# A Mamba block with projections in split precision: two of the next unit's four x tiles are made in a unit's first part, and the last lowering of g moves into the next unit

## The reference

```python
proj = jnp.einsum('bsd,ed->bse', x, in_proj_w)      # gate 8192 | x 8192, B 1024, C 1024 | dt 128
hBC  = silu(causal_conv(proj_hBC, conv_w, taps=4) + conv_b)
L    = exp(segsum(dt * A))                          # per head, within a chunk
Y_diag = einsum('bzlhn,bzshn,bhzls,bzshp->bzlhp', C, B, L, x * dt)
Y_off  = einsum('bzlhn,bzhpn,bhzl->bzlhp', C, prev_states, exp(A_cum))
y = Y_diag + Y_off + x * D
g = y * silu(gate)
g = g * rsqrt(mean(g * g over a group's 1024 channels) + eps) * norm_w
out = einsum('bsi,oi->bso', g, out_proj_w)
```

## Time and profile before

| what | value |
|---|---|
| median of 3 runs | 1887.01 us |
| profiled execution | 1886.13 us, span 1884.3 us |
| granted TensorE clock, mean | 0.982 |
| PE busy | 1778.5 us, 94% |
| VectorE busy | 1293.8 us, 69% |
| ScalarE busy | 1061.2 us, 56% |
| GpSimd busy | 935.5 us, 50% |
| DMA | 114.14 MB, 61 GB/s |

### The profile page before, as it was taken

The page is one execution under the profiler, slowest core; times in us unless marked ns, Lnnn a source line. Parts: engine busy times, 40 slices in busy tenths (PEclk is TensorE's granted clock), DMA queues, the critical chain, the costliest instruction groups (busy, mean ns, idle before and its releaser), DMA issues.

```text
span 1884.3 us, 31309 instructions
## 1 busy us (share of the span) xinstructions
PE 1778.5 (94%) x9752; PEld 1375.2 (73%) x9752; DVE 1293.8 (69%) x2091; ACT 1061.2 (56%) x1936; POOL 935.5 (50%) x717
## 2 busy tenths in 40 slices
PE   7989999999999999999999999999999999999976
PEld 6867778777777777777777777777777777777755
DVE  4756667666666677766676667666677666766688
ACT  5546555656546566555546565465665555565632
POOL 1325464555445565354645554454654545455563
PEclk9799999999999999999999999999999999999988
DMA  4412121111202121022211212121211212112121
GB/s 175 156 41 71 55 65 49 40 62 53 71 28 71 49 67 50 26 71 59 67 45 44 62 48 71 31 68 49 68 50 31 66 60 65 43 47 62 34 95 56
DMA packets 77162, 114.14 MB, mean 61 GB/s; under 512 B 21441, under 2 KB 28097, under 8 KB 76097
## 3 DMA queue, kind: packets, MB, share of 16 engines
q1 hardware_dynamic: 59424, 80.07, 14.4%
q10 hardware_dynamic: 17568, 31.99, 5.2%
HBM read 88.94 MB, written 23.07 MB: 59 GB/s over the span
## 4 chain that ended last, share of the span: by engine, by line
issue 46%; POOL 34%; PE 9%; DVE 5%; ACT 3%; SPq 1%; DMA 1%; POOLq 1%; ACTq 0%; DVEq 0%
POOL yt L1509 9%; POOL ssq L1504 6%; POOL wg_lo L1440 4%; POOL wo_lo L1440 4%; POOL prev L1490 3%; POOL yt L1512 3%; POOL wx_lo L1440 3%; PE bank L454 2%; PE bank L456 2%; PE bank L455 2%; PE bank L591 1%; PE bank L654 1%; ACT lm L999 0%; DMA acc<-x_dram 0%; DVE bn L1095 0%
## 5 line engine op out<-in xcount | busy, mean ns | idle before, releaser
L1509 POOL TENSOR_TENSOR yt<-yt,ea 128x384 f32<-128x384 f32 (+1 forms) x128 | 189.3, 1479 | 392.4 <-DVE ea L1356 392.4
L1145 DVE SCALAR_TENSOR_TENSOR xc<-bank,bpar,xc 128x511 f32<-128x511 f32 (+2 forms) x384 | 285.7, 744 | 52.7 <-ACT xc L854 48.2
L1326 DVE TENSOR_TENSOR lm<-lm,cbm 128x512 f32<-128x512 f32 x256 | 186.4, 769 | 158.4 <-ACT lm L1002 158.4
L454 PE MATMUL bank<-h_hi,wg_hi 128*128 128x512 f32 x640 | 264.7, 414 | 27.8 <-ACT gate L958 17.6
L456 PE MATMUL bank<-h_hi,wg_lo 128*128 128x512 f32 x640 | 252.5, 395 | 0.0
L455 PE MATMUL bank<-h_lo,wg_hi 128*128 128x512 f32 x640 | 251.9, 394 | 0.0
L454 PE MATMUL bank<-wo_hi,g_hi 128*128 128x512 f32 x496 | 207.7, 419 | 7.2 <-POOL wo_lo L1440 7.2
L1490 POOL TENSOR_TENSOR prev<-prev,dec 128x512 f32<-128x512 f32 x96 | 101.8, 1061 | 221.7 <-DVE prev L1275 130.7
L454 PE MATMUL bank<-h_hi,wx_hi 128*128 128x512 f32 x512 | 210.7, 411 | 0.0
L456 PE MATMUL bank<-h_hi,wx_lo 128*128 128x512 f32 x512 | 201.0, 393 | 0.0
L455 PE MATMUL bank<-h_lo,wx_hi 128*128 128x512 f32 x512 | 200.6, 392 | 0.0
(11 more groups left out here) (180 smaller groups left out, 3836.7 us busy)
## 6 DMA issues: line engine op xcount, KB each, us to landing
raw_w<-w_in_dram SPq DMA_DIRECT2D x145, 256.0 KB, 2.7
raw_w<-w_out_dram SPq DMA_DIRECT2D x64, 256.0 KB, 2.6
part_d<-part ACTq DMA_DIRECT2D x64, 256.0 KB, 2.2
part<-part_d ACTq DMA_DIRECT2D x58, 256.0 KB, 2.7
rt<-rows_d SPq DMA_DIRECT2D x256, 8.0 KB
acc<-x_dram SPq DMA_DIRECT2D x8, 256.0 KB, 6.8
acc<-w_mod_dram SPq DMA_DIRECT2D x2, 1024.0 KB, 6.1
lh<-neg_d SPq DMA_DIRECT2D x128, 8.0 KB
```

The lines of the kernel that those rows point to most:

```text
L454: nc.tensor.matmul(out_ap, whi(k), hhi(k), start=(k == 0), stop=False)
L1145: stt(dst[:, at], ps[:, 0:HALF - 3 + k], w(k), dst[:, at], ALU.mult, ALU.add)\
L1326: tt(lm[:, h % 4, :], lm[:, h % 4, :], cbm[:, toks(hf)], ALU.mult).then_inc(v_m, 1)
L1509: tt(yt[:, j % 2, cols], yt[:, j % 2, cols], ea[:, j % 2, cols], ALU.add).then_inc(p_t3, 1)
```

## The change

The x tiles are projected in the order 2, 3, 0, 1. Tiles 2 and 3 of the next unit are projected, tapped, convolved and put through Silu in the first part of a unit. For this `xc` has six slots instead of four (tiles 2 and 3 alternate), and `prev` four instead of five. Only two x tiles (for c = 3: the four B/C half tiles and two x tiles) stay in the second part. For c > 0, `transposes(0)` comes ahead of gate tile 1. `lower_g` of the last pair is done by VectorE after the second scaling of x in the next unit. The fills' order and their places in the first part change too. The core of the diff, with the parts for the prologue, the indices and the last unit left out:

```diff
-        xc = sb("xc", [128, NCT, HALF])
+        xc = sb("xc", [128, NCT + 2, HALF])
-        prev = sb("prev", [128, NZ + 1, BLOCK])
+        prev = sb("prev", [128, NZ, BLOCK])
...
+        X_ORDER = (2, 3, 0, 1)
+        def x_fill(c, j):
+            return 4 + nth(j) if c == 1 else (16, 17, 20, 21)[nth(j)]
...
         def by_step(todo):
             if len(todo) == 6:
-                return [todo[0:1], todo[1:3], todo[3:4], todo[4:6]]
-            return [todo[z:z + 1] for z in range(4)]
+                return [todo[0:2], todo[2:3], todo[3:5], todo[5:6]]
+            return [todo[0:2], todo[2:3], todo[3:4], []]
...
             if c == 3:
-                return [[("bc", 0), ("bc", 1)], [("bc", 2), ("bc", 3), ("x", 0)], [("x", 1), ("x", 2)], [("x", 3)]]
-            return [[("x", j)] for j in range(NCT)]
+                return [[("bc", 0), ("bc", 1)], [("bc", 2), ("bc", 3)], [("x", 0)], [("x", 1)]]
+            return [[], [("x", 0)], [("x", 1)], []]
...
 TensorE, gate_proj
-                if z == 2:
-                    te.wait_ge(a_gate, 4 * u + (2 if c == 0 else 1))
-                else:
-                    te.wait_ge(v_conv, 4 * u + (2, 3, 0, 4)[z])
+                if z == 0 and c == 0:
+                    te.wait_ge(v_bcconv, 4 * (g + 1))
+                    te.wait_ge(v_conv, 4 * u + 2)
+                elif z == 0:
+                    te.wait_ge(a_ea, 4 * (u - 1) + 1)
+                elif z == 1:
+                    te.wait_ge(v_conv, 4 * u + (3 if c == 0 else 4))
+                elif z == 2 and c == 0:
+                    te.wait_ge(v_conv, 4 * u + 4)
+                elif z == 2:
+                    te.wait_ge(a_gate, 4 * u + 1)
...
+                else:
+                    te.wait_ge(v_conv, 4 * (u + 1) + 1)
...
 TensorE, the unit (before: gates 1 and 2, then per z transposes, out_proj, states, gate 3 at z = 2)
+                def next_work(j):
+                    if c == 3:
+                        if j < 2:
+                            next_bc(2 * j)
+                            next_bc(2 * j + 1)
+                        else:
+                            next_x(j - 2)
+                    elif j < 2:
+                        next_x(j)
+                    elif j == 2:
+                        gate_proj(g, c + 1, 0)
...
                 if c == 0:
                     gate_proj(g, c, 0)
+                    gate_proj(g, c, 1)
                     group_bc()
+                    transposes(0)
+                    transposes(1)
+                else:
+                    transposes(0)
+                    gate_proj(g, c, 1)
+                    transposes(1)
                 gate_proj(g, c, 2)
+                previous(0)
+                states(0)
+                transposes(2)
+                next_x(2)
+                previous(1)
+                states(1)
+                transposes(3)
+                next_x(3)
+                gate_proj(g, c, 3)
+                previous(2)
+                states(2)
+                exp_a(0)
+                diff(0)
+                diff(1)
+                previous(3)
...
 ScalarE, the unit's first part (new order)
+                for f in todo[0]:
+                    unit_fill(f, g)
+                if c == 0:
+                    silu_gate(u, c, 0)
+                silu_gate(u, c, 1)
+                for f in todo[1]:
+                    unit_fill(f, g)
+                silu_gate(u, c, 2)
+                for f in todo[2]:
+                    unit_fill(f, g)
+                if more:
+                    next_tap(("x", 2))
+                part_step(0)
+                if more:
+                    silu_x(u + 1, hv, 2)
+                part_step(1)
+                if more:
+                    next_tap(("x", 3))
+                silu_gate(u, c, 3)
+                if more:
+                    silu_x(u + 1, hv, 3)
...
 ScalarE, second part, behind split_g(j - 1), the taps and the fill of j
+                    if more and c < 3:
                         if j == 2:
+                            silu_x(u + 1, hv, 0)
+                        if j == 3:
+                            silu_x(u + 1, hv, 1)
+                            silu_gate(u + 1, c + 1, 0)
...
 VectorE, the unit's first part (new order)
+                scale_x(0)
+                scale_x(1)
+                if not first:
+                    lower_g(u - 1, (c - 1) % UPG, NCT - 1)
+                    group_sums(u, g1, b1, h1)
+                new_state(0)
+                scale_x(2)
+                previous(0)
+                next_conv(("x", 2))
+                previous(1)
+                new_state(1)
+                scale_x(3)
+                next_conv(("x", 3))
+                previous(2)
+                new_state(2)
```

More of the change, by code:

```diff
@@ L269, in ffn_bank @@
             return (6, 7, 4, 5)[t % 4]
[L271 to L275, removed]
         block = ctx.enter_context(nc.Block())
@@ L609, in exp_a @@
                 def exp_a(j):
-                    if j == 0:
+                    if j == 0 and end:
                         te.wait_ge(a_gate, 4 * u + 3)
+                    elif j == 0:
+                        te.wait_ge(v_conv, 4 * (u + 1) + 2)
                     elif j == 1:
@@ L653, in transposes, with previous @@
                     for j in range(NCT):
-                        lst = nc.tensor.transpose(bank[2 + z % 2][:, j * 128:(j + 1) * 128], xc[:, j, chunk(z)],
+                        lst = nc.tensor.transpose(bank[2 + z % 2][:, j * 128:(j + 1) * 128], xc[:, xslot(hf, j), chunk(z)],
                                                   ident[:, :])
                     lst.then_inc(t_xt, 1)
+                def previous(z):
+                    if first or (end and z > 0):
+                        return
+                    if z == 0 and hf == 1:
+                        te.wait_ge(p_w, filled(g, 3 if c == 1 else 15))
+                    out_proj(u - 1, z)
+                    if z == 0:
+                        if c == 0:
+                            te.wait_ge(v_bl, 2 * g + 1)
+                        if c in (0, 3):
+                            sum_squares(g - 1 if c == 0 else g, 1 if c == 0 else 0)
@@ L1019, in split_g @@
                     act(g_parts(not more)[0][:, j, :], yt[:, j % 2, :], ACT.Copy, scale=par(c // 2, j, NORM)).then_inc(a_hi, 1)
-                    if j == NCT - 1 and not (last and c == 3):
-                        silu_x(u + 1, 3)
                     if c < 2 and j == 0:
@@ L1068, in unit @@
                 split_g(NCT - 1)
+                if more and c == 3:
+                    silu_x(u + 1, hv, 1)
             def group(g, last, first):
@@ L1308, in unit, with previous @@
-                    if end and z == 3:
-                        ve.wait_ge(a_bcsilu, 2 * GROUPS)
-                        for v in range(2):
-                            for k in range(NK):
-                                i = 16 + v * NK + k
-                                ts((ga_row, gb_row)[v][:, k * 128:(k + 1) * 128], ident[:, :], small[:, i:i + 1], None,
-                                   ALU.mult).then_inc(v_diag, 1)
-                items, n = proj_items(c, last), 0
+                def previous(z):
+                    if not first and not (end and z > 0):
+                        accumulate(u, g1, b1, h1, z)
@@ L1318, in unit, with next_conv, lower_g @@
+                items = proj_items(c, last)
                 nv, hv = (nb, 1) if hf == 0 else (nb + 1, 0)
                 pv = (c // 2) if hf == 0 else (c // 2 + 1) % 2
+                def next_conv(item):
+                    if not end:
+                        conv(item, item_bank(c, item), nv, hv, g + 1, pv)
+                def lower_g(v, cv, j):
+                    ve.wait_ge(a_hi, 4 * v + j + 1)
+                    ghi, glo = g_parts(end and cv == c)
+                    if j == 0 and not (end and cv == c):
+                        ge(ve, t_out, 4 * v)
+                    stt(glo[:, j, :], yt[:, j % 2, :], par(cv // 2, j, NORM), ghi[:, j, :].bitcast(F),
+                        ALU.mult, ALU.subtract).then_inc(v_lo, 1)
@@ L1321, in mix @@
+                if end:
+                    ve.wait_ge(a_bcsilu, 2 * GROUPS)
+                    for v in range(2):
+                        for k in range(NK):
+                            i = 16 + v * NK + k
+                            ts((ga_row, gb_row)[v][:, k * 128:(k + 1) * 128], ident[:, :], small[:, i:i + 1], None,
+                               ALU.mult).then_inc(v_diag, 1)
                 def mix(h):
```

255 lines of the change are left out of this document (110 added, 145 removed).

## The result

The changed kernel takes 2096.86 us (median of 4 runs, 2092.37 to 2099.92) against 1885.87 us (4 runs, 1883.68 to 1892.02) of the kernel before on the same chip: 1.111 times as long, 95% interval [1.108, 1.113]. The forecast was 2053 us, the range 1950 to 2105.

The account below looks back on a forecast made before the run. The prediction took TensorE, busy 94% of the span, as the bound, with at most 7.6 us per group to win. It summed 1886 + 132 (waits) + 35 (clock) = 2053 us, range 1950 to 2105.

Parts of the forecast that it names:

- The waits: New TensorE waits at yo, yd, transposes, group_bc and gate 3: 25.5 us per middle group together.
- behind group_bc and ahead of out_proj: In c = 0, 1.0 us of wait for mask products and 1.0 us for the last lowering of g.
- the saved changes of kind: On TensorE, a projection behind another saves 0.1 us; four saved per group, 0.4 us.
- the largest term: For c > 0, transposes wait 4.0 to 4.1 us for the last x tile's Silu; 12.1 us per group.
- 18 falls, times 1.7: TensorE's clock falls at 18 of 24 transposes waits, 1.7 us each: 31 us; clock term +35 us in all.
- The chain behind yo: Second part bound at 6.7 to 6.8 us per pair through GpSimd, ScalarE and VectorE, against TensorE's 5.50 us.
- 7.6 us per group: TensorE's idle time in a middle group of the kernel before, taken off the new waits.
- rival (4): Last Silu early, transposes don't wait, 6.0 + 0.4 us per group won: 1835 us, chance 0.05.
- Costs put at nothing: Lowering g late is harmless; table loads stay two per unit at 1.28 us, without the skill's 1.4 us drain.
- (1): The waits come as forecast and TensorE's clock holds: 2018 us, chance 0.24.
- (2): Only the transposes wait, TensorE being late enough at yo, with half the clock falls: 1955 us, chance 0.10.
- (3): Something not followed in the first part waits too, 1 to 2 us per unit: 2100 us, chance 0.12.

Follow-up runs that it names:

- Experiment 1: Changed kernel with gate tile 1 projected ahead of transposes(0) for c > 0, transposes(1) following at once: 2008.98 us, 1.065 times the kernel before.
- experiment 5: Changed kernel with ScalarE doing Silu of x tile 1 at j = 3 ahead of split_g(2), its Square and the fill: 2007.57 us, 1.062 times the kernel before.
- experiment 6: Kernel before with only transposes(0) put ahead of gate tile 1 for c > 0: 2051.23 us, 1.085 times the kernel before.
- experiment 10: Changed kernel with ScalarE's and VectorE's B/C items in c = 3 spread as 1, 2, 1 and an x tile: 2070.62 us, ratio 1.096.
- experiment 12: Kernel before with eight unneeded matmuls ahead of gate tile 1 in each unit with c > 0: 1892.69 us against 1887.57, 1.002.
- experiment 2: Changed kernel with eight unneeded matmuls of 512 columns ahead of transposes(0) in each unit with c > 0: 2050.37 us, 1.086 times the kernel before.
- experiment 7: Changed kernel with gate tile 1 ahead of transposes(0) and a third ea buffer together: 1990.68 us, 1.053 times the kernel before.
- Experiment 4: Changed kernel with a third ea buffer for c = 0 to 2: 2071.85 us, 1.098 times the kernel before.
- experiment 9: Kernel before with Silu of the next unit's gate tile 0 moved ahead of split_g(2) at j = 3: 1888.50 us against 1887.57, 0.999.
- experiment 11: Changed kernel with the last lowering of g back at the end of its own unit on VectorE: 2093.04 us, 1.109 times the kernel before.

## Why the prediction was right, and where its size was off

**The waits: right, place by place.** For one middle group, new and old waits by the trace (forecast in brackets): yo of c = 0, 1.5 (1.2); of c = 1, 0.4 + 0.8 + 1.7 = 2.9 (2.6); of c = 2, 0.35 + 2.6 = 2.9 (1.5); of c = 3, 3.6 and yd 1.0 (3.7 and 1.2); the transposes 3.9, 4.0, 3.2 (4.0 to 4.1 each, 12.1); gate 3 in c = 3, 0.7 (1.2); behind group_bc and ahead of out_proj, 0.6 (2.0). Sum 24.3 us (25.5). The idle time grew by 16.7 us per group (17.9 without the saved changes of kind), and by 131 us over the span (132). That the sum fits so well is in part luck: c = 2 was 1.4 us too low, group_bc and out_proj 1.4 too high. Experiments 1, 5 and 6 show the largest term by removing and by adding it alone, experiment 10 the one of c = 3.

**The clock: right in sign, less than half in size.** "18 falls, times 1.7" is the term that was mis-sized. The prediction made it 35 us in all, 4.4 per group; TensorE's busy time grew by 10.4 per group, times eight 83 us. That is 48 us more, and the miss is 44. Both factors were small. The clock fell at every place, the yo of c = 3 included, four per group. And a fall cost about 10.4 / 4 = 2.6 us, not 1.7. At the place shown it cost 3.2: ten slow matmuls of gate 1 at 0.20 us each, 0.7 in yd, 0.5 in the transposes; where it fell inside the wait, yd lost nothing. The prediction took its price from a fall with one wait ahead of it and long projections behind. There the low clock lasted some 3 us (1149 to 1152); here, with short products, a second wait and the gate in a row, it lasted 7 us (12 of the 24 places at the transposes, and c = 3 in the middle groups) or 10 us (the 11 places where it fell in yd). Experiment 1 takes the second wait out of the row, and a fall costs 2.0 us again.

Busy time is not all lost time, though. The 0.7 us in yd stand inside the 5.97 us that the last Silu sets, and the wait behind is shorter by as much (3.2 instead of 3.9), at the 11 places. And a group has 14 waits now against 10, each with a little busy time that its row doesn't have (experiment 12). So what the clock costs in time is 1 to 2 us per group less than 10.4, by this estimate, and still twice the forecast. The split rests on one profiled execution of each kernel. Experiments 1, 2 and 5 bear out that the clock is a large part, and experiment 7 comes nearest to the waits without it: 85 of its 103 us are idle time.

**The chain behind yo: right in length, wrong as the only bound.** The forecast named one chain of 6.7 to 6.8 us through GpSimd's t3. From copy to copy a pair took 6.4 us in c = 0, where t3 and t1 have 384 columns, and 6.8 in c = 1 (1170.66 to 1177.47). Experiment 4 shows VectorE's list beside it, at 6.3, which the prediction did not sum.

**What was removed: the waits went, the gain did not come from them.** The prediction counted 7.6 us per group off. It is so in the sum of rows; experiments 9 and 12 show that in the kernel before most of them were time behind one queue, so that rival (4), which priced them at 51 us, would probably not have come true even with an early Silu. This was not tested on the changed kernel. The bound of 7.6 us per group was itself low: each of the 10 waits behind it cost up to 0.27 us beyond its row.

**Costs put at nothing.** The lowering of g (experiment 11) and the table loads held: the Silu starts 0.01 us behind the load of 1.28 us (1125.60, 1126.89), and the load 0.02 us behind the fill ahead of it (1124.92 + 0.66). The drain that the Trainium skill adds ("ScalarE: Activation LUTs", "What ACT_TABLE_LOAD costs") does not show here either; none of the changed kernel's 67 loads has more than 0.08 us of idle time ahead of it or 0.01 behind.

**Rivals.** (1), the clock holds, at 2018 us: falsified by the group's clock of 0.94 and 10.4 us more busy time. (2), only the transposes wait: falsified by yo's 86.7 us. (3) had nearly the right time (2100) for a wrong reason: in the first part only 0.6 us, and 0.7 at gate 3 of c = 3, are new, where it had 4 to 8 per group.

## What to carry to other kernels

Before work is moved between stages, follow the list of each in-order engine to the instruction that the moved consumer needs, and price the wait from there: this gave each wait to within 1.5 us, and the sum per group to within 1.2. A consumer of the last link of a chain belongs behind independent long work (here one gate projection, worth 88 us), and its producer ahead of anything in its queue that is not urgent (one Silu, 89 us). Where waits fall between short matmuls, price the clock by how long it stays down behind them, and count all waits in a row as one place. The sum of waits behind one producer's queue is no gain to be had by serving one of them earlier (experiment 9).

## What the runs showed of the hardware

- **Useless matmuls made a kernel faster**, by 46 us for 192 of them (experiment 2), and cost only 5 us where the engine waited anyway (experiment 12).
- **VectorE's and GpSimd's operations take longer where they overlap.** A pair of mask products takes 1.29 us where GpSimd is idle (1105.76 in the changed kernel; GpSimd starts again at 1112.43), 1.54 where they overlap for part, and 2.38 to 2.40 us in experiment 4. GpSimd there, same columns:

```profile
975.40 1.84 POOL L1538 TENSOR_TENSOR wo_lo<-raw_w,wo_hi 128x512 fp32r<-128x512 f32 x1
978.99 1.45 POOL L1610 TENSOR_TENSOR yt<-yt,ea 128x384 f32<-128x384 f32 x1 [1.75 <-DVE ea L1455]
...
981.76 1.78 POOL L1605 TENSOR_TENSOR ssq<-ssq,sq 128x512 f32<-128x512 f32 x1
...
985.30 1.44 POOL L1610 TENSOR_TENSOR yt<-yt,craw 128x384 f32<-128x384 f32 x1
```

A low part takes 1.84 us and a sum of squares 1.78 beside them; at the end of the same unit, with VectorE idle for most of it, they take 1.30 (at 994.53) and 1.29 (at 993.29). By the Trainium skill ("SBUF — State Buffer", "SBUF: two separate sides") a VectorE operation with both inputs in SBUF and a GpSimd operation that reads SBUF exclude each other. The rows agree in that both grow, but no run took one of the two away. So 1.1 us of VectorE's 6.33 us per pair (2.40 - 1.29) seem to be this.
- **A short wait costs TensorE more than its idle time**: 0.27 us beyond the row in the place shown under experiment 12, for matmuls of 512 columns that otherwise overlap.
- **A wait costs more clock where another wait follows**: the low clock lasted some 3 us behind the wait of 2.04 us in the kernel before, and 7 to 10 us at the ends of units in the changed one.
